# Where the layer norm's shift is added: into the transposed context, or behind its projections

## What is computed

```python
x  = _layernorm(tgt, ln1_g, ln1_b)          # tgt: 8 x 224 x 512
...                                         # self-attention, 16 heads, causal
result = tgt + sa_out
xq = _layernorm(result, ln2_g, ln2_b)
xs = _layernorm(src, ln2_g, ln2_b)          # src: 8 x 750 x 512
kv = xs @ ed_wkv                            # 512 x 1024
k2, v2 = (_heads(t) for t in jnp.split(kv, 2, axis=-1))
q2 = _heads(xq @ ed_wq)
wei2 = jax.nn.softmax(jnp.einsum('bhtd,bhjd->bhtj', q2, k2) * scale, axis=-1)
ed_out = _merge(jnp.einsum('bhtj,bhjd->bhtd', wei2, v2)) @ ed_wproj + ed_bproj
result = result + ed_out
h = jax.nn.relu(_layernorm(tgt, ln3_g, ln3_b) @ ff_w1 + ff_b1)
result = result + (h @ ff_w2 + ff_b2)
```

## Time and profile before

| | before |
|---|---|
| median of 3 runs | 1353.84 us |
| profiled execution, its own time | 1353.37 us |
| its span in the trace | 1351.3 us |
| mean granted clock of TensorE | 0.993 of full speed |
| TensorE busy | 1299.2 us |
| VectorE, GpSimd, ScalarE busy | 787.9, 699.9, 663.2 us |

### The profile page before, as it was taken

One profiled execution on the slowest core, in us unless ns is written; L12 is line 12 of the kernel. 1 busy time (PEld: TensorE's weight loads), 2 busy tenths in 40 slices (PEclk: granted clock), 3 DMA queues, 4 the chain that ended last, 5 costly groups with the idle time before them and its releaser, 6 DMA issues.

```text
span 1351.3 us, 24602 instructions
## 1 busy us (share of the span) xinstructions
PE 1299.2 (96%) x9193; PEld 1074.6 (80%) x9193; DVE 787.9 (58%) x2003; ACT 663.2 (49%) x1611; POOL 699.9 (52%) x582
## 2 busy tenths in 40 slices
PE   6999999999999999999898999999999999999997
PEld 6888888888878888888787787878778787887874
DVE  6712223223677777776655575756657575675575
ACT  5411111222666766566625456564655647456444
POOL 3233131323434664559653767675676756667661
PEclk9999999999999999999998999999999999999999
DMA  7400102113657575697577666768667577766641
GB/s 236 142 28 16 63 32 71 41 61 112 132 156 204 146 187 146 162 225 212 157 133 126 117 94 115 131 114 139 95 137 111 104 131 125 124 101 108 92 71 42
DMA packets 102128, 160.06 MB, mean 118 GB/s; under 512 B 10389, under 2 KB 63421, under 8 KB 100730
## 3 DMA queue, kind: packets, MB, share of 16 engines
q1 hardware_dynamic: 102010, 158.50, 55.8%
HBM read 70.93 MB, written 28.31 MB: 73 GB/s over the span
## 4 chain that ended last, share of the span: by engine, by line
PE 82%; POOL 6%; DVE 5%; issue 3%; ACT 2%; DMA 2%; SPq 0%; POOLq 0%; ACTq 0%; DVEq 0%
PE ps L1777 20%; PE ps L164 13%; PE ps L453 12%; PE ps L423 10%; PE ps_pair L1794 6%; PE ps L1809 6%; PE ps L1823 5%; PE ps L1886 3%; POOL ca_partial L1639 2%; POOL ca_xT L1518 2%; PE ps L1246 1%; PE ps L1266 1%; PE ps_pair L1236 1%; PE ps L1841 1%; DMA ca_k_stack<-ca_keys 1%
## 5 line engine op out<-in xcount | busy, mean ns | idle before, releaser
L1716 DVE TENSOR_REDUCE ca_maxes<-ps 112x1 f32<-112x375 f32 x512 | 256.9, 540 | 112.9 <-PE ps L1809 110.8
L1660 ACT ACTIVATE ca_probT<-ps_pair 125x448 f32<-125x448 f32 x384 | 210.3, 554 | 180.3 <-PE ps_pair L1794 178.4
L1639 POOL TENSOR_TENSOR ca_partial<-ca_partial,ca_probT 125x896 f32<-125x896 f32 x118 | 249.3, 2112 | 93.6 <-ACT ca_probT L1660 88.9
L312 POOL TENSOR_TENSOR ff_hT<-ff_hrelu,ff_hT 128x512 fp32r<-128x512 f32 (+1 forms) x64 | 78.8, 1233 | 203.3 <-DVE ff_hT L394 203.3
L1809 PE MATMUL ps<-ca_k_stack,ca_q_stack 96*112 96x376 f32 x512 | 167.8, 352 | 4.0 <-DVE ca_mrow L1744 2.1
L1794 PEld LDWEIGHTS ps_pair<-ca_q_stack,ca_k_stack 98*125 98x125 f32 x768 | 130.2, 186 | 44.0 <-issue 31.9
L1794 PE MATMUL ps_pair<-ca_q_stack,ca_k_stack 98*125 98x224 f32 x768 | 156.2, 285 | 1.3 <-ACT ca_probT L1660 1.2
L423 PE MATMUL ps<-ff_w,ff_hT 128*128 128x512 f32 x672 | 155.5, 390 | 0.0
L1777 PE MATMUL ps<-ca_xT,w_a 128*128 128x376 f32 x768 | 154.3, 337 | 0.2 <-issue 0.2
L1777 PE MATMUL ps<-w_b,ca_xT 128*125 128x512 f32 x576 | 151.6, 400 | 2.5 <-POOL ca_xT L1518 2.5
L423 PEld LDWEIGHTS ps<-ff_w,ff_hT 128*128 128x128 f32 x672 | 125.6, 188 | 25.8
(11 more groups left out here) (144 smaller groups left out, 2406.2 us busy)
## 6 DMA issues: line engine op xcount, KB each, us to landing
ca_k_stack<-ca_keys SPq DMA_DIRECT2D x96, 376.0 KB, 8.0
sa_Q_stack<-sa_rows SPq DMA_DIRECT2D x96, 112.0 KB, 3.6
sa_K_stack<-sa_rows SPq DMA_DIRECT2D x96, 112.0 KB, 3.7
ca_q_stack<-q_out SPq DMA_DIRECT2D x96, 112.0 KB, 9.4
ctx_tokens<-in_ctx_dram SPq DMA_DIRECT2D x14, 672.0 KB
ctx_tokens<-in_L_xattn_ff_w_dram SPq DMA_DIRECT2D x16, 512.0 KB, 4.4
q_out<-sa_yT SPq DMA_DIRECT2D x16, 448.0 KB, 4.1
wp_lo<-wp_out SPq DMA_DIRECT2D x6, 1024.0 KB, 4.8
```

What stands on the lines that cost most here:

```text
L312: pool.tensor_tensor(hT[:, LO, m % RING, 0:width(g)], hrelu[i % 2][:, 0:width(g)], hT[:, HI, m % RING, 0:width(g)].bitcast(F32), ALU.subtr ...
L1639: pool.tensor_tensor(total, total, half(a), ALU.add).then_inc(partial_done, 1)
L1660: act.activation(probT[u // GH][0:JT, u % GH].rearrange("p a t -> p (a t)"), ps_p[u % 2][0:JT, 0:2 * T], ACT.Exp).then_inc(exp_done, 1)
L1716: dve.tensor_reduce(maxes[:, q, j, a:a + 1], ps_s[n % 3][0:TQ, 0:JH], AX_X, ALU.max).then_inc(s_read, 1)
```

## The change

- **T.** ScalarE makes one pass instead of two, with the gain alone. VectorE makes the low half straight from the bank of PSUM (bank times gain, less the high half), and this frees the bank. `ca_xT_f` and GpSimd's L1518 are gone, and so is the shift: it is not in `ca_xT` any more. TensorE's K and V wait for VectorE's reads of the T banks.
- **Padding.** The padding column of `ca_xT` now holds the shift, split in halves by GpSimd.
- **Keys.** Column 375 of the keys' product is so the product of the weights by the shift, one number per partition. ScalarE copies it into `key_beta` once for each quarter of heads, adds it in the high half (an ACTIVATE in place of a CAST), and VectorE adds it in the low half.
- **Values.** The rows of the probabilities sum to one after normalisation, so the values' part of the shift can be added to the attention output. It comes from four new products "beta" of 12 matmuls each, with `w_b` as weights and two columns to multiply, which stand in four slots of `EARLY`; ScalarE copies one column of each. ScalarE and VectorE add it when they split the attention output.
- **Attention output.** Its low half is VectorE's in all quarters, where GpSimd had 28 of the 32.

```diff
     (-8, BEFORE): [turned(3, 0)],
-    (-8, BEHIND): [turned_rest(3, 0)],
+    (-8, BEHIND): [turned_rest(3, 0), ("beta", 0, 0)],
     (-7, BEFORE): [turned(0, 1)],
-    (-7, BEHIND): [turned_rest(0, 1)],
+    (-7, BEHIND): [turned_rest(0, 1), ("beta", 0, 1)],
...
-    (-4, BEHIND): [turned_rest(3, 1)],
+    (-4, BEHIND): [turned_rest(3, 1), ("beta", 0, 2)],
     (-3, BEFORE): [("context", 1, 1)],
+    (-3, BEHIND): [("beta", 0, 3)],
...
             items += scores[:1]
+            items += late
             items += fill[i]
-            items += late
...
-xT_f32 = sb("xT_f32", [P, KT, 2, JP], F32, 6144 + 4 * KT * 2 * JP)
...
+            eng.scalar_tensor_tensor(piece[:, LO, t], full[:, t], value_beta[:, G % KT:G % KT + 1],
+                                     piece[:, HI, t].bitcast(F32), ALU.add, ALU.subtract).then_inc(olo_done, 1)
-
-    def context_low(eng, b, m, a):
-
-        wait_acc_read(eng, "T", b, m, a)
-        eng.tensor_tensor(xT[:, LO, m, a, 0:JH], xT_f32[:, m, a, 0:JH],
-                          xT[:, HI, m, a, 0:JH].bitcast(F32), ALU.subtract).then_inc(xlo_done, 1)
+    def wait_turned(pe, b, a):
+        for m in range(KT):
+            wait_acc_read(pe, "T", b, m, a)
...
-            pool.memset(xT[:, :, :, :, JH:JP].bitcast(F32), 0.0).then_inc(constants_ready, 1)
+            split_exactly(pool, cn["one"], xT[:, HI, :, :, JH], xT[:, LO, :, :, JH],
+                          beta.unsqueeze(2).to_broadcast([P, KT, 2]), pad_hi, 1).then_inc(constants_ready, 1)
...
-        if name == "T_rest":
-            context_low(pool, *item[1:])
-        if name == "D_low" and item[1] < NG - KT:
-            result_low(pool, item[1])
...
-                act.copy(oT[G % PIECES][:, HI, t], oT_f32[G % PIECES][:, t]).then_inc(ohi_done, 1)
+                act.activation(oT[G % PIECES][:, HI, t], oT_f32[G % PIECES][:, t], ACT.Identity,
+                               bias=value_beta[:, G % KT:G % KT + 1]).then_inc(ohi_done, 1)
+        if name == "beta":
+            g = item[2]
+            wait_acc_psum(act, *item)
+            act.copy(value_beta[:, g:g + 1], acc_of(*item)[:, 0:1]).then_inc(acc_read(*item), 1)
...
-            act.copy(keys[:, HI, a], acc[:, 0:JP]).then_inc(khi_done, 1)
+            g = G % KT
+            if G < KT and a == 0:
+                act.copy(key_beta[:, g:g + 1], acc[:, JH:JP]).then_inc(key_beta_done, 1)
+                act.wait_ge(key_beta_done, g + 1)
+            act.activation(keys[:, HI, a], acc[:, 0:JP], ACT.Identity, bias=key_beta[:, g:g + 1]).then_inc(khi_done, 1)
...
             act.activation(xT[:, HI, m, a, 0:JH], acc[:, 0:JH], ACT.Identity,
-                           bias=cn["columns"][:, 3 * KT + m:3 * KT + m + 1],
-                           scale=cn["columns"][:, 2 * KT + m:2 * KT + m + 1]).then_inc(xhi_done, 1)
-            act.activation(xT_f32[:, m, a, 0:JH], acc[:, 0:JH], ACT.Identity,
-                           bias=cn["columns"][:, 3 * KT + m:3 * KT + m + 1],
-                           scale=cn["columns"][:, 2 * KT + m:2 * KT + m + 1]).then_inc(acc_read(*product), 1)
+                           scale=gain[:, m:m + 1]).then_inc(xhi_done, 1)
...
-        if name == "D_low" and item[1] >= NG - KT:
+        if name == "D_low":
             result_low(dve, item[1])
...
-            dve.tensor_tensor(keys[:, LO, a], acc_of("K", G, a)[:, 0:JP], keys[:, HI, a].bitcast(F32),
-                              ALU.subtract).then_inc(acc_read("K", G, a), 1)
+            dve.scalar_tensor_tensor(keys[:, LO, a], acc_of("K", G, a)[:, 0:JP], key_beta[:, G % KT:G % KT + 1],
+                                     keys[:, HI, a].bitcast(F32), ALU.add, ALU.subtract).then_inc(acc_read("K", G, a), 1)
+        if name == "T_rest":
+            _, b, m, a = item
+            dve.wait_ge(xhi_done, turned_number(b, m, a))
+            dve.scalar_tensor_tensor(xT[:, LO, m, a, 0:JH], acc_of("T", b, m, a)[:, 0:JH], gain[:, m:m + 1],
+                                     xT[:, HI, m, a, 0:JH].bitcast(F32), ALU.mult, ALU.subtract)\
+                .then_inc(acc_read("T", b, m, a), 1)
...
             if (g, part) == (0, 0):
-                pe.wait_ge(xlo_done, XT * b + XT // 2 * (a + 1))
+                wait_turned(pe, b, a)
...
+        if name == "beta":
+            g = item[2]
+            if g == 0:
+                sa.wait(pe, "value_weights")
+                pe.wait_ge(constants_ready, 1)
+            mm = whole_product(pe, acc[:, 0:2], lambda c, k: wv[:, c, k, P * g:P * (g + 1)], lambda c, k: xT[:, c, k, :, JH])
```

More of the change, by code:

```diff
@@ L133, in key @@
             return item[:5]
-        return item[:4] if name in ("K", "V", "E") else None
+        return item[:4] if name in ("K", "V", "E", "beta") else None
     def bank(self, key):
@@ L1467, in cross_attention @@
     shift = sb("shift", [JT, NT], F32, 6112)
+    key_beta, value_beta = (sb(n, [P, KT], F32, offset) for n, offset in (("key_beta", 38272), ("value_beta", 38304)))
+    gain, beta = cn["columns"][:, 2 * KT:3 * KT], cn["columns"][:, 3 * KT:4 * KT]
+    pad_hi, key_beta_done, value_beta_done = sem("pad_hi"), sem("key_beta_done"), sem("value_beta_done")
     res_landed, wp_landed, out_stored = sem("res_landed"), sem("wp_landed"), sem("out_stored")
@@ L1475, in cross_attention @@
     ohi_done, olo_done, wp_lo_landed = sem("ohi_done"), sem("olo_done"), sem("wp_lo_landed")
-    khi_done, mhi_done, xhi_done, xlo_done, shift_done = (
-        sem(n) for n in ("khi_done", "mhi_done", "xhi_done", "xlo_done", "shift_done"))
+    khi_done, mhi_done, xhi_done, shift_done = (
+        sem(n) for n in ("khi_done", "mhi_done", "xhi_done", "shift_done"))
     NG = KT * B
@@ L1512, in result_low, with turned_number @@
             eng.wait_ge(ohi_done, n)
-            eng.tensor_tensor(piece[:, LO, t], full[:, t], piece[:, HI, t].bitcast(F32), ALU.subtract).then_inc(olo_done, 1)
-    def context_low(eng, b, m, a):
-        wait_acc_read(eng, "T", b, m, a)
-        eng.tensor_tensor(xT[:, LO, m, a, 0:JH], xT_f32[:, m, a, 0:JH],
-                          xT[:, HI, m, a, 0:JH].bitcast(F32), ALU.subtract).then_inc(xlo_done, 1)
+            eng.scalar_tensor_tensor(piece[:, LO, t], full[:, t], value_beta[:, G % KT:G % KT + 1],
+                                     piece[:, HI, t].bitcast(F32), ALU.add, ALU.subtract).then_inc(olo_done, 1)
+    def turned_number(b, m, a):
+        return XT * b + KT * a + m + 1
+    def wait_turned(pe, b, a):
+        for m in range(KT):
+            wait_acc_read(pe, "T", b, m, a)
     def sums_of(G, pair):
@@ L1772, in vector @@
                 .then_inc(acc_read("E", b, m), 1)
+    whole_product = product
     def half_product(pe, part, acc, lhs, rhs):
@@ L1842, in tensor @@
             mm.then_inc(d_psum, 1)
-        if name not in ("K", "V", "T", "E"):
+        if name not in ("K", "V", "T", "E", "beta"):
             return
-        product = item if name == "T" else item[:3]
+        product = item if name in ("T", "beta") else item[:3]
         acc = acc_of(*product)
-        if name == "T" or item[-1] == 0:
+        if name in ("T", "beta") or item[-1] == 0:
             banks.wait_free(pe, ("ca",) + product)
@@ L1863, in tensor @@
             if (t, part) == (0, 0):
-                pe.wait_ge(xlo_done, XT * b + XT // 2)
+                wait_turned(pe, b, 0)
             mm = half_product(pe, part, acc[0:JT, :],
@@ L1887, in tensor @@
                                start=(part, i) == (0, 0), stop=(part, i) == (KT - 1, len(PASSES) - 1))
-        if name == "T" or item[-1] == (3 if name == "E" else 1):
+        if name in ("T", "beta") or item[-1] == (3 if name == "E" else 1):
             mm.then_inc(acc_psum(*product), 1)
```

## The result

The changed kernel takes 1365.06 us, the median of 4 runs (1364.32 to 1366.32), against 1354.55 us (4 runs) before: a ratio of 1.0073, interval 1.0059 to 1.0087. It is slower by 8 to 12 us. I had forecast 1357.5 and a range up to 1364; the sign was right and the size far off.

The account below looks back on a forecast made before the run. It took TensorE, busy 96% of the span, as the bound. Burst -0.7, shift's products +4.4, keys +0.2 and attention output 0.0 gave +3.9 on 1353.37, so 1357.3, stated as 1357.5 us; range 1352 to 1364.

Parts of the forecast that it names:

- The burst: Context transpositions of batches 1 to 7: TensorE's wait passes to VectorE, 0.1 us less per burst, 0.7 over seven.
- The shift's own products: End of self-attention: four times 12 two-column matmuls, with lost and swallowed waits, add 4.4 us.
- The products: Four two-column products at the weight-load pitch of 12 matmuls, 1.42 us each, 5.7 us in all.
- The bank of the output projection: First product takes the bank VectorE reads until 651.1; scores and transposes move behind that wait, + 0.7 us.
- The waits that I took as swallowed: TensorE's waits at 653.25 (0.91), 662.04 (1.43) and 0.5 of the 0.63 at 660.08 take up 2.8 us of delay.
- Rival 2: Existing waits swallow the shift's products: + 0.7 us or none, 1353.7, no change; chance 0.08.
- The terms of + 0.2 and + 0.6: Third product waits for a low half, + 0.2 us; its ScalarE copy precedes the queries' projection copies, + 0.6.
- My upper bound of 8 us: Shift's products cost 8 us if the new 2.1 us wait lets the clock fall while weight-bound products run.
- Keys and attention output: Longer key passes hidden behind the next quarter's products, 0.2 us; VectorE's attention-output low half hidden, 0.0.
- Rival 1: Bursts really open, VectorE's operations overlapping better and TensorE left alone: -6.4 us, 1347; chance 0.12.
- Rival 3: VectorE is the slower pacer in the bursts, low half 0.7 us or more: +7, 1364; chance 0.18.
- Rival 4: VectorE's two-SBUF-source attention-output low half is held up by GpSimd's sums of probabilities: 28 us, 1385; chance 0.05.

Follow-up runs that it names:

- odd shared: Changed kernel with the shift as a row of the values' product, odd column blocks by two ScalarE passes and GpSimd's low half: 1353.03 us, 0.9989 of before.

## Why the prediction was wrong

**The burst: right.** Forecast: the wait changes its owner to VectorE and keeps nearly its length, 0.1 us less. Measured: 0.05 more, the same three places. VectorE's low half has a pitch of 0.51 (910.13 to 910.64), I took 0.53; its slot is 1.42, I said 1.45.

**The shift's own products: the step that failed.** The forecast was 5.7 + 0.7 + 0.2 + 0.6 - 2.8 = 4.4, the stretch gives 11.3. The failing sentence is "I let it fall once in either kernel". The clock fell twice and stayed down for 6.8 and 10.2 us, not once for 3.4. Item by item:
- The products: 1.36 + 2.56 + 2.30 + 2.56 = 8.8, against 5.7. The pitch at full clock was right; three of four ran at 1.2 GHz.
- The last two and what stands among them: from 662.04 to the keys' product at 665.15 it was 3.1 us, from 667.75 to 677.92 it is 10.2. Of the 7.1 more, 4.9 are two products and 2.2 are scores, transposes and probabilities at half their speed, which had no term at all. In the first half of the stretch such work adds another 0.5.
- The bank of the output projection: 0.7 us of other work moved behind the wait, as forecast; the wait grew by 0.5, from 1.33 to 1.83.
- The waits that I took as swallowed: 0.91 at 653.25 is gone, but 1.43 at 662.04 became 1.64 and 0.63 stayed 0.63. Of 2.8 us, 0.7 was given back. Rival 2's counter-argument (waits for VectorE come later when TensorE does) was right, and I hadn't applied it to my own sum.
- The terms of + 0.2 and + 0.6: TensorE shows no wait for either.

Together: the products 8.8, other work at the lower clock 2.7, and the waits 0.2 less (4.1 for 4.3), which is 11.3.

My upper bound of 8 us for this term did name the cause, the clock falling behind the new wait while weight-bound products run. It was too small because it had the clock down for the products alone; the trace has it at 0.50 for everything that stands between and behind them too, until a keys' product is under way. Why it stays down so long, and what sets off each fall, the runs don't settle; the width of the products is one condition (3.4 us with 224 columns).

**Keys and attention output: right that they are hidden.** ScalarE's pass is 0.574 (0.472 before), VectorE's half 0.606 (0.549), and the kernels without the products measure 1.0007 and 1.0009. The last group's low half adds 0.06 (the final output projection waits 2.57, 2.51 before).

**Rival 1** (the burst opens) did not happen, but it was nearer than I put it. My condition for it was VectorE's amount of work per slot; the place of the low half in the slot gives 7 us at the same amount. **Rival 3**'s time, 1364, was met for another reason. **Rival 4** didn't occur in the changed kernel (no attention output's low half over 0.46 us) and did in the odd shared one, there from GpSimd's low half and not from its sums.

The Trainium skill, SBUF — State Buffer, "Who interferes with whom", gives that exclusion; the 0.90 us of the odd shared kernel agree with it. So does the gain when the pair was parted, though only 0.46 of its 0.79 us a burst can be the exclusion's. The half throughput that the Trainium skill, Vector Engine (DVE) Microarchitecture Reference, "Points that are easy to get wrong", gives a scalar-tensor-tensor instruction with two SBUF sources isn't seen: 0.446 us for 224 columns, 0.388 for the plain subtraction of the last quarters before. With a PSUM source the same step to the three-operand form costs as much, 0.606 against 0.549. The measurement decides: 0.06 us more, not 0.23.

## What to carry to other kernels

Small products are not cheap products: twelve matmuls of 128x128 weights cost 1.4 us whether they have two columns or 224, and at the end of self-attention, among stalls and other narrow work, the narrow ones kept TensorE at 1.2 GHz for 17 us in place of 3.4, and the four cost 8 to 12 us. Between products of 512 columns the same four cost 4.6, and as one more column of weights in a product that is there anyway nothing that could be measured. When the granted clock is down in a trace, cost the work around the new instructions at the lower level as well. And when a wait goes from one engine to another without getting shorter, look first at the order in the new engine's queue: the operation that frees what TensorE waits for goes ahead of those that can wait.

## What I had not expected of the hardware

- TensorE was busy for 8.99 of the 9 us from 669 to 678, and the granted clock stood at 0.50 all that time. With 224 columns in the same products it stood there for 3.4 us of the whole stretch, not 17, and with the two-column products between wide ones it did not fall beside them.
- The same stretch without these products had the clock at 0.50 for 0, 3.4, 6.8 or 10.2 us in nine traced executions, behind stalls of much the same length (0.9 to 1.8 us). The stretch is 45.9 to 47.4 us long without a fall and 49.4 with 10.2 us of it.
- A ScalarE pass with one number per partition is followed by the next operation after 0.46 us, with two after 0.55, so an operand that is not needed is worth 0.09 us a pass.
